# L1's probabilities of seven heads turned by DVE and through DRAM, with other orders in the prologue, the last heads and FFN1

## The reference

```python
x = x + L0_xattn(layernorm(x), ctx)   # 16 query heads, 4 kv heads of 96, keys from ctx and x
x = x + L0_ffn(layernorm(x))          # relu^2 MLP, routed low-rank part, layer norm
x = x + L1_xattn(layernorm(x), ctx)   # 32 query heads, 8 kv heads of 128, keys from ctx
x = x + L1_ffn(layernorm(x))

def L1_xattn(query, kv):              # 8 kv heads, 4 query heads each (G)
    q = query @ Wq + bq
    k, v = split(kv @ Wkv + bkv)
    attn = softmax(q k^T / sqrt(128))
    return concat(attn @ v) @ Wo + bo

def L1_ffn(x):                        # H = x W^T + b; z = x A; gates from every second token
    weights = normalised(probs * sigmoid((probs - second_largest) / 0.5))
    return H + ((z * (repeat(weights, 2) @ LiMEs)) @ Bmat) * 0.5
```

## Time and profile before

| | us |
|---|---|
| median of 3 runs | 1121.05 (1119.25 to 1121.1) |
| profiled execution | 1119.5 |
| its span, first to last instruction | 1117.7 |
| TensorE busy | 1086.7 (97%) |
| DVE busy | 553.4 (50%) |
| ACT busy | 532.9 (48%) |
| POOL busy | 377.9 (34%) |

### The profile page before, as it was taken

One profiled execution on the slowest core, in us unless ns is written; L12 is line 12 of the kernel. 1 busy time (PEld: TensorE's weight loads), 2 busy tenths in 40 slices (PEclk: granted clock), 3 DMA queues, 4 the chain that ended last, 5 costly groups with the idle time before them and its releaser, 6 DMA issues.

```text
span 1117.7 us, 14762 instructions
## 1 busy us (share of the span) xinstructions
PE 1086.7 (97%) x5246; PEld 882.7 (79%) x5246; DVE 553.4 (50%) x1018; ACT 532.9 (48%) x1478; POOL 377.9 (34%) x260
## 2 busy tenths in 40 slices
PE   5999999999999999999999999999999999999997
PEld 4888888887877688877888888888888888888775
DVE  4465356347477443385534435345254353543654
ACT  5475367257478332456525436244262451733641
POOL 3053034024253453476503306024051240512441
PEclk9999999999999999999999999999999999999999
DMA  8111001010000221102121121120211202111002
GB/s 247 29 45 32 1 29 29 1 42 15 1 19 1 104 95 38 38 1 76 39 97 54 38 75 38 58 93 31 82 38 52 98 19 94 38 47 50 8 10 76
DMA packets 41998, 55.22 MB, mean 49 GB/s; under 512 B 20484, under 2 KB 32004, under 8 KB 39268
## 3 DMA queue, kind: packets, MB, share of 16 engines
q1 hardware_dynamic: 41956, 54.67, 15.0%
HBM read 44.69 MB, written 5.77 MB: 45 GB/s over the span
## 4 chain that ended last, share of the span: by engine, by line
PE 89%; ACT 5%; DVE 4%; issue 1%; POOL 1%; DMA 0%; SPq 0%; ACTq 0%; DVEq 0%
PE work L630 15%; PE work L631 14%; PE work L632 14%; PE work L689 8%; PE yb L630 5%; PE yb L632 5%; PE yb L631 5%; PE pt L702 3%; PE ov L630 3%; PE ov L632 3%; PE ov L631 3%; PE pt L632 3%; PE pt L631 3%; PE pt L630 3%; ACT prob L1163 2%; DVE oT_lo L1713 1%
## 5 line engine op out<-in xcount | busy, mean ns | idle before, releaser
L1390 POOL TENSOR_TENSOR prob<-prob,exp_rcp 128x512 f32<-128x512 f32 (+1 forms) x96 | 127.2, 1325 | 528.3 <-DVE exp_rcp L1642 528.3
L1163 ACT ACTIVATE prob<-work,neg_max 128x128 f32<-128x128 f32 (+1 forms) x384 | 149.1, 407 | 65.1 <-DVE neg_max L1667 64.9
L630 PE MATMUL work<-xT_hi,q_hi 128*128 128x512 f32 x416 | 168.1, 404 | 0.4 <-DVE xT_lo L1749 0.4
L632 PE MATMUL work<-xT_hi,q_lo 128*128 128x512 f32 x416 | 164.4, 395 | 0.0
L631 PE MATMUL work<-xT_lo,q_hi 128*128 128x512 f32 x416 | 164.4, 395 | 0.0
L689 PE MATMUL work<-kT,qT 128*128 128x128 f32 (+1 forms) x704 | 112.9, 303 | 0.1
L689 PEld LDWEIGHTS work<-kT,qT 128*128 128x128 f32 (+1 forms) x704 | 102.8, 191 | 11.8 <-issue 0.3
L1119 ACT ACTIVATE oT_hi<-ov 32x128 fp32r<-32x128 f32 (+2 forms) x160 | 60.2, 376 | 99.0 <-PE ov L632 96.5
L1713 DVE TENSOR_TENSOR oT_lo<-ov,oT_hi 32x128 fp32r<-32x128 f32 (+2 forms) x160 | 67.4, 421 | 74.7 <-ACT oT_hi L1119 73.3
L1667 DVE TENSOR_REDUCE neg_max<-work 128x4 f32<-128x512 f32 (+1 forms) x96 | 82.9, 863 | 39.7 <-PE work L689 37.8
L630 PE MATMUL yb<-o_hi,oT_hi 128*128 128x512 f32 x224 | 93.4, 417 | 5.1 <-DVE oT_lo L1713 5.1
(11 more groups left out here) (219 smaller groups left out, 2112.2 us busy)
## 6 DMA issues: line engine op xcount, KB each, us to landing
raw<-in_l_q SPq DMA_DIRECT2D x8, 1024.0 KB, 5.5
raw<-in_l_o SPq DMA_DIRECT2D x8, 1024.0 KB, 4.7
kv_raw<-in_l_kv SPq DMA_DIRECT2D x8, 515.0 KB, 3.4
prob<-vT SPq DMA_DIRECT2D x128, 32.0 KB, 1.8
p_bounce<-bo_bc SPq DMA_DIRECT2D x14, 256.0 KB, 2.1
prob<-p_bounce SPq DMA_DIRECT2D x56, 64.0 KB, 2.0
raw<-in_l_o SPq DMA_DIRECT2D x4, 768.0 KB, 4.2
raw<-in_l_q SPq DMA_DIRECT2D x16, 144.0 KB, 2.6
```

The lines of the kernel that those rows point to most:

```text
L630: pe.matmul(dst, l_hi, r_hi, start=first and k == 0, stop=False)
L632: mm = pe.matmul(dst, l_lo, r_hi, start=False, stop=last and k == n - 1)
L1163: e = act.activation(prob[:, i % 2, g * L.keys:(g + 1) * L.keys], s[:, g, :], ACT.Exp, bias=neg_max[:, i % 2, g:g + 1], accum_out=exp_sum[ ...
L1390: pool.tensor_tensor(p, p, exp_rcp[:, b % 2, :].unsqueeze(2).broadcast_to([P, G, L.keys]), ALU.mult)\
```

## The change

All elements of the first seven L1 heads go by DVE, DRAM and back, and none of them by `transpose_p`. Each engine has a new program for these heads, `turned_head`, of NB + 4 steps, in which `values` and `output` come one step later than before. v comes back into vT in place of `prob`; the returned probabilities use the upper half of `prob`. SP moves element 0 ahead of the o load and the others behind it, and POOL's `o_lo` follows the scaling of element 1. Elements 6 and 7 had this way before.

```diff
+            def move_p(it, b):
+                sp.wait_ge(p_turned, it * NB + (b + 1))
+                sp.dma_start(bounce[b % 2], bo_bc[:, :]).then_inc(p_out, 16)
+                sp.wait_ge(p_out, it * (NB * 16) + 16 * (b + 1))
+                if b >= 2:
+                    sp.wait_ge(S1.pt_lo_done, it * NB + (b - 1))
+                blocks = bounce[b % 2].rearrange("(i t) (j c) -> j t i c", t=third, j=4)
+                for j in range(4):
+                    dst = prob[third * j:third * (j + 1), b % 2, HID:2 * HID].rearrange("t (i c) -> t i c", i=4)
+                    sp.dma_start(dst, blocks[j]).then_inc(p_back[b % 2], 16)
...
+                move_p(it - 1, 0)
                 load(o_raw[:, :], A["l1_o"][it], o_loaded, o_lo_done, it + L1.o0)
-                move_p(it - 1)
+                for b in range(1, NB):
+                    move_p(it - 1, b)
                 move_v(it)
```

TensorE's new head (`TURN_AHEAD` spreads the eight projections of the next head over four steps, 3, 2, 2 and 1):

```diff
+            def turned_head(L, S, it):
+                for i in range(NB + 4):
+                    if i >= NB:
+                        for kind, u in TURN_AHEAD[i - NB]:
+                            project(L, S, it + 1, kind, u)
+                    if i == 2:
+                        project(L, S, it, "q", 6)
+                        project(L, S, it, "q", 7)
+                    if i == 3:
+                        values(L, S, it, 0)
+                    if i > 4:
+                        output(L, S, it, i - 4, (0, 1))
+                    if i < NB:
+                        scores(L, S, it, i)
+                    if i == 4:
+                        output(L, S, it, 0, (0, 1))
+                    if i == 0:
+                        pe.wait_ge(N[2].lo, NB)
+                    if i < 2:
+                        project(L, S, it, "q", 4 + i)
+                    if NB <= i:
+                        output(L, S, it, i - 4, (2, 3))
+                    if 4 <= i < NB + 3:
+                        values(L, S, it, i - 3)
+                    if 4 <= i < NB:
+                        output(L, S, it, i - 4, (2, 3))
```

ACT and DVE (their helpers first):

```diff
+            def back_upper(S, it, b):
+                act.wait_ge(p_back[b % 2], it * (NB * 32) + 64 * (b // 2 + 1))
+                act.activation(p_of(pT_hi[:, 0, :]), p_back_of(b), ACT.Copy).then_inc(S.pt_hi_done, 1)
...
+            def turned_head(L, S, it, next_kv, next_q):
+                for i in range(NB + 4):
+                    if i >= NB:
+                        evacuate(L, S, it + 1, *TURN_AHEAD[i - NB])
+                    if i == 2:
+                        evacuate(L, S, it, ("q", 6))
+                    if 3 <= i < NB + 3:
+                        back_upper(S, it, i - 3)
+                    if i == 3:
+                        act.wait_ge(S.act_evac, L.evacuated(it, "q", 6))
+                    if i in (3, 4, 5):
+                        next_weights(L, S, it, i, None, next_kv, next_q)
+                    if 3 <= i < NB + 3:
+                        oT_upper(L, S, it, i - 3)
+                    if i < NB:
+                        exponentials(L, S, it, i)
+                    if i == 0:
+                        evacuate(L, S, it, ("q", 4))
+                        upper_v(S, it)
+                        split_hi(o_hi, o_raw, 0, L.tiles * HID, P, o_loaded, S.scores_done, it + L.o0, it * NB + 1)\
+                            .then_inc(o_hi_done, 1)
...
             def turn_p(S, it, b):
                 dve.wait_ge(S.norm_done, it * NB + (b + 1))
-                if b == TURNED[1]:
-                    dve.wait_ge(p_out, it * 32 + 16)
+                if b:
+                    dve.wait_ge(p_out, it * (NB * 16) + 16 * b)
...
+            def back_lower(S, it, b):
+                dve.wait_ge(S.pt_hi_done, it * NB + (b + 1))
+                dve.tensor_tensor(p_of(pT_lo[:, 0, :]), p_back_of(b), p_of(pT_hi[:, 0, :]).bitcast(F32), ALU.subtract)\
+                    .then_inc(S.pt_lo_done, 1)
+
+            def turned_head(L, S, it):
+                for i in range(NB + 4):
+                    if i >= 5:
+                        add_share(L, S, it, i - 5, None)
+                    if i < 3 and i:
+                        turn_p(S, it, i - 1)
+                    if i == NB:
+                        turn_p(S, it, NB - 1)
+                    if i >= NB:
+                        evacuate(L, S, it + 1, *TURN_AHEAD[i - NB])
+                    if i == 2:
+                        evacuate(L, S, it, ("q", 7))
+                    if 3 <= i < NB + 3:
+                        back_lower(S, it, i - 3)
+                    if 3 <= i < NB:
+                        turn_p(S, it, i - 1)
+                    if i < NB:
+                        negative_max(L, S, it, i, False)
+                    if 3 <= i < NB + 3:
+                        oT_lower(L, S, it, i - 3)
+                    if i < NB:
+                        dve.wait_ge(S.exp_done, it * NB + (i + 1))
+                        dve.reciprocal(exp_rcp[:, i % 2, :], exp_sum[:, i % 2, :]).then_inc(S.rcp_done, 1)
+                    if i == 0:
+                        lower_v(S, it)
+                    if i == 1:
+                        evacuate(L, S, it, ("q", 5))
+                add_share(L, S, it, NB - 1, None)
```

POOL takes x's rows in the last head of each attention, and `o_lo` moves:

```diff
+            def normal_rows(n, b):
+                rstd_of(n, b)
+                pool.wait_ge(n.rstd, b + 1)
+                if b >= n.bufs:
+                    pool.wait_ge(n.t, b - n.bufs + 1)
+                pool.tensor_scalar(xn_buf(n, b), x[:, b, :], mean_var[:, b, 0:1], rstd[:, b:b + 1],
+                                   ALU.subtract, ALU.mult).then_inc(n.xn, 1)
...
                     if norm is not None and b >= 4:
-                        rstd_of(norm, b - 4)
+                        normal_rows(norm, b - 4)
                     normalise(L, S, it, b)
-                    if b == 0:
+                    if b == (1 if L.double and norm is None else 0):
                         split_lo(o_of(L)[1], o_raw, o_of(L)[0], L.tiles * HID, P, o_hi_done, o_lo_done, it + L.o0)
```

The prologue: five products on a tile that DVE fills with ones come first on TensorE, the x transposes stand elsewhere between the context products, ACT evacuates kv 0 and kv 2 and splits q in another order, POOL splits q in two parts:

```diff
+            pe.wait_ge(warm_set, 1)
+            for _ in range(5):
+                pe.matmul(ov[:, :], kT[:, 0:P], kT[:, 0:HID], start=True, stop=True)
...
             for u in range(4):
                 project_context(u, [2, 3], False, True).then_inc(S0.proj_done, 1)
-                transpose_x(N[0], u, ())
+                for b in ((0,), (1,), (2, 3), ())[u]:
+                    transpose_x(N[0], b, ())
...
+            for b in range(4):
+                normalise_x(N[0], b, x[:, b, :])
+            for b in range(4):
+                norm_hi(N[0], b)
+            evacuate(L0, S0, 0, ("kv", 0))
+            act.wait_ge(q_parts_loaded, (2 * KT - 1) * 16)
+            split_hi(q0_hi, q_raw, 0, 1536, P, q_loaded, None, 0, 0).then_inc(q_hi_done, 1)
+            evacuate(L0, S0, 0, ("kv", 2))
+            normalise_x(N[0], 4, x[:, 4, :])
```

FFN1's end: two of the chained DVE steps go (a factor 0.5 that moves into ACT's exponential, and a factor 1.0), wT and p_mix are made by halves in two banks each, and the `delta` products stand between the parts of the last H product:

```diff
-        DELTAS = (6, 7, 4, 5, 0, 1, 2, 3)
-        BY_DVE = DELTAS[2:]
+        DELTAS = (4, 5, 6, 0, 1, 7, 2, 3)
+        BY_DVE = (4, 5, 0, 1, 2, 3)
+        MOVED = (6, 7)
...
+            for b in DELTAS[:3]:
+                delta(b)
+            big_h(7, (1, 2))
+            for b in DELTAS[3:5]:
+                delta(b)
+            big_h(7, (3,))
+            for b in DELTAS[5:]:
+                delta(b)
```

More of the change, by code:

```diff
@@ L611, in _ @@
                 sp.dma_start(b_raw[rows, :], A["Bmat"]).then_inc(ffn1_loaded, 16)
[L612 to L619, removed]
+            for b in (4, 5, 0, 6, 1, 2, 3, 7):
+                if b in MOVED:
+                    sp.wait_ge(f1.moved_done, MOVED.index(b) + 1)
+                else:
+                    sp.wait_ge(f1.done, BY_DVE.index(b) + 1)
                 sp.dma_start(out[b], x[:, b, :]).then_inc(out_stored, 16)
@@ L1021, in _, with delta @@
             big_h(5)
-            big_h(6, (0, 1))
+            big_h(6, (0,))
             pe.wait_ge(f1.w, 1)
[L1025 to L1031, removed]
+            for n, half in enumerate((1, 0)):
+                for c in (2 * half, 2 * half + 1):
+                    mm = pe.transpose(wT_bank(half)[:, c % 2 * P:(c % 2 + 1) * P], lg[5][:, c, :], ident[:, :])
+                mm.then_inc(f1.wT, 1)
+            for n, half in enumerate((1, 0)):
+                big_h(6, (n + 1,))
+                pe.wait_ge(f1.wT_evac, n + 1)
+                pe.matmul(pmix_bank(half), limes[:, :], wT[:, half * 2 * P:(half + 1) * 2 * P], start=True, stop=True)\
+                    .then_inc(f1.pmix, 1)
+            big_h(6, (3,))
+            big_h(7, (0,))
             pe.wait_ge(f1.b_lo, 1)
-            for b in DELTAS:
+            def delta(b):
                 pe.wait_ge(f1.zp_again, 1 if b >= 4 else 2)
@@ L1102, in split_v3, with pT_upper @@
                         .then_inc(S.v_hi_done, 1)
[L1104 to L1109, removed]
+            def pT_upper(L, S, it, b):
                 for c in range(L.sources):
-                    by_pe = NB * L.sources - (len(TURNED) if L.double else 0)
```

(21 more changed lines are left out.)

167 lines of the change are left out of this document (78 added, 89 removed).

## The result

The changed kernel takes 1170.53 us (median of 4 runs, 1168.95 to 1171.32); the kernel before took 1120.15 beside it. The ratio is 1.0448, 95% interval 1.043 to 1.0466: 50 us slower. 1152 was forecast, with a range to 1168. The direction and the two waits came as predicted; several sizes did not. The profiled execution took 1171.32 (span 1169.5), so its rows stand for the median.

A forecast was written before the change was run, and what follows sets the result against it. Full TensorE was taken to bound L1 heads. Each of seven would lose 7.65 + 0.7 - 2.62 = 5.75 us; 1119.5 + 40.2 - 8.5 = 1151.2, plus half the median gap: 1152 us (1143 to 1160; wider 1131 to 1168).

The forecast's parts named there:

- So the three loop steps lose little; with their start I give them 0.7: Turned L1 heads, steady steps: DVE's 4.49 us per element against TensorE's 4.4, so 0.7 us lost per head.
- back_lower 0.65: DVE's remainder of a returned tile in a turned head was priced at 0.65 us, from a trace row.
- POOL has the room: Last heads of L0 and L1: POOL takes scaling of x's rows from ACT, gaining 2.5 us in each.
- What is taken away: Six of eight transposed blocks leave TensorE in seven L1 heads: 2.62 us per head, 18.3 in all.
- First wait: TensorE stands 3.74 us before values(0), because ACT's copy and DVE's remainder of element 0 come behind element 2's work.
- Second wait: Output(0) waits until 21.8 us for out(1) behind the 1 MB load; at values(1) TensorE is 7.65 us behind.
- that rival: Turned heads: the 1 MB load does not delay out(1) and the clock stays up; 1134 us, chance 0.19.
- 4.7 plus a quarter of its moving time: Time allowed for out(1) to land behind the 1 MB load: the load's 4.7 us plus 0.7, landing at 19.65.
- The loop after that: Turned heads after values(1): per element TensorE wants 4.4 us, DVE 4.49, SP 3.8; 0.7 us lost per head.
- The clock: After the 3.74 us idle the clock falls to its low level, hidden before output(0) at 21.8; nothing added.
- the rival of a lasting low level: Turned heads: the low clock reaches past values(1), adding 2.2 us per head; 1167 us, chance 0.13.
- The other edits: Outside the turned heads: prologue -2 us, POOL's rows in two last heads -2.5 each, FFN1's end -1.5; -8.5 together.

The follow-up runs named there:

- the run of the heads alone: Turned heads put into the kernel before, without the prologue, POOL's rows or FFN1 edits: 1174.61 us, ratio 1.048.
- the run of the first wait alone: Changed kernel with ACT's copy and DVE's remainder of element 0's returned tile moved ahead of element 2's exponentials and maximum: 1166.48 us, ratio 1.0404.
- the two repairs together: Changed kernel with the output weights' load behind all transfers, and element 0's copy and remainder ahead of element 2's exponentials and maximum: 1160.95 us, ratio 1.0365.

## Why the prediction came out low

The prediction had the two waits, their places and their releasers. What failed first is the step behind them, "So the three loop steps lose little; with their start I give them 0.7", and in it the term "back_lower 0.65": a remainder took up to 1.32 beside POOL's scaling, and a loop step 4.92. Two long heads and "POOL has the room" make the rest. One by one:

- **What is taken away** held: 24 instructions fewer a head.
- **First wait**: place and releaser right, 4.29 for 3.74. The term that was off is "back_lower 0.65": that row was taken while POOL was idle. Here it stands for POOL's scaling, 1.32.
- **Second wait**: right in place and cause, and in size partly by luck. With t = 0 at 759.83, out(1) landed at 19.93 (19.65 forecast), output(0) started at 21.96 (21.8), values(1) at 24.79 (24.35). The load does hold it up (with the load moved, every transfer out of that head lands 2.0 to 2.1 after its issue); that rival fell. But from the load's issue to the landing "4.7 plus a quarter of its moving time" made 5.40, and 5.97 was measured; the load was issued 0.29 earlier than forecast, which hid half of that.
- **The loop after that** failed in size: 4.92 for 4.49. The sum of DVE's own instructions does not set the step; a chain across the engines does (below). Of the 0.43 a step, 0.2 is the remainder's contention (4.92 to 4.72 when it reads PSUM). With 0.44 more at values(1), a head is 1.45 above the forecast 77.05, 10 us in seven heads.
- **Two heads of 82.6 and 83.0** were in no case. There a remainder stood 2.83 and 2.86 for a split of POOL that had begun just before it; TensorE waited 2.3 and 3.3, and the low level followed. 4.1 and 4.4 us more: 8 in all. The traces agree elsewhere: the run of the heads alone has one remainder of 2.56 and the run of the first wait alone one of 2.88, each in its one head of over 82, and no head without such a remainder takes more than 80.2 in any trace. With the remainder reading PSUM the second is a steady head and the first 1.6 above.
- **The clock**: the low level came where it was said, and was hidden where it was said (products in the wait change the steady heads by 0.1). But it was hidden with little to spare: scores 4 ended at 21.6 (20.7 forecast), 0.4 before output(0), and it took the transfer's place as soon as that was gone. That the time lies near the rival of a lasting low level (1167) is chance: in the steady heads output(0) and values(1) run at full clock.
- **The other edits** (-8.5 forecast, -6.4 measured): the prologue gave 2.95 (first maximum of L0 at 50.17, 53.12 before; -2 forecast), the way from there to L1's first scores, with L0's last head in it, 1.7 (-2.5), L1's last head up to FFN1's small products 2.1 (-2.5), and FFN1's end lost 0.35 (-1.5). The step "POOL has the room" failed: a row is 2.1, not at most 1.04, so POOL's last addition ends where it did before against the head's start, and the all-reduce gives back 1.85 of what the rows and the new end gain.

Together 10 + 8 + 2 = 20: the profiled execution's 1171.3 against the sum's 1151.2.

What is left of the loop step once the contention is gone, DVE and TensorE in the run of the kernel as changed with the remainder reading PSUM:

```profile
782.34 0.69 DVE L1837 TENSOR_TENSOR oT_lo<-ov,oT_hi 128x512 fp32r<-128x512 f32 x1 [0.56 <-ACT oT_hi L1171]
```

```profile
783.17 0.47 PE L641 MATMUL yb<-o_hi,oT_hi 128*128 128x512 f32 x1
```

There the remainder is done at 785.08, and the next `values` starts at 785.46, behind TensorE's own scores: DVE no longer holds it. TensorE stands about 0.3 a step before the first half of `output`: from `values` it has six products (1.4 us) to do, while ACT's copy of oT and DVE's remainder of it take until 783.03. The prediction had no term for this chain. It is read from the trace, not tried.

A rule for the remainder is in the Trainium skill (SBUF — State Buffer, section Who interferes with whom): a DVE instruction with two SBUF inputs contends with a POOL instruction that reads SBUF, the port pair that they share is an exclusive lock, and issue order decides who blocks. The trace agrees, with its 0.54 to 0.55 after POOL's end in each case and 0.68 to 0.69 with one operand in PSUM. For the all-reduce's 5.5 us the Trainium skill has a rule near it too (GPSIMD Engine Reference, section 2.1 Instruction dispatch): a freshly loaded routine's first call pays about 6 us with no instruction to be seen. The 5.5 to 5.6 of "issue" here fits; that code loading is the cause no run shows.

## What to carry to other kernels

Work taken from a full engine is only a gain if nothing that engine then waits for got longer: price each replacement as it runs beside its new neighbours, and read its row from a stretch where the other engines are as busy as they will be. Where two delays end at nearly the same place, mending one shows next to nothing in the period; mend both, and keep the engine's clock up, before judging the idea. For a loop, follow one result across all engines until it comes round, besides adding up each engine's own work. Before work is given to an engine because it idles, look at the next thing that waits for that engine's last instruction.

## What the runs showed that was not expected

- POOL's scaling of one 128x512 row by two scalars of a partition takes 2.08 to 2.10 us, twice the 1.04 of its two-input scaling of the same size.
- A transfer of 256 KB issued 0.48 us behind a 1 MB load on the same queue landed after 5.5 us, alone after 2.0.
- Two waits of 1.70 and 2.76 us, with work at full clock between them, were followed by the low level about 1 us into the next work in the two repairs together, as the one of 4.29 is in the kernel as changed.
- The part from the last head's first maximum to the end is the same program in all ten kernels with the turned heads and the side edits. It takes 95.6 to 95.9 us in eight traces, 98.7 with the load alone moved and 100.4 in the kernel as changed with the remainder reading PSUM: in these two the granted clock is 0.50 for 6 us and more at FFN1's end. What made it fall there is open.
